# Decoder layer on one core: the second attention's key and value weights split inside the first attention, its first key and value projections at the first attention's end

## The reference, cut to what matters

```python
q = (x @ Wq).reshape(b, t, KV, G, D); k = (x @ Wk).reshape(b, t, KV, D); v = (x @ Wv).reshape(b, t, KV, D)
w = softmax(where(causal_mask, einsum('bqhgd,bkhd->bhgqk', q, k) * scale, -inf))
x2 = norm(x + einsum('bhgqk,bkhd->bqhgd', w, v).reshape(b, t, H * D) @ Wo)
Q = (x2 @ xWq.T + bq).reshape(bs, sl, H, HD)
K = (ctx @ xWk.T + bk).reshape(bs, sl, H, HD); V = (ctx @ xWv.T + bv).reshape(bs, sl, H, HD)
x3 = norm(x2 + einsum('bshg,bsgd->bshd', softmax(einsum('bshd,bsgd->bshg', Q, K)), V) @ xWo.T + bo)
```

## Time and profile before

| | |
|---|---|
| median of 3 runs | 1992.71 us (1992.0 to 1996.39) |
| profiled execution | 1994.85 us |
| its span, first to last instruction | 1992.8 us |
| TensorE busy | 1866.1 us (94%) |
| VectorE, ScalarE, GpSimd busy | 1143.3, 688.5, 262.8 us |
| granted TensorE clock, mean | 0.979 |
| first attention | from 0 to about 343 us |
| second attention | about 343 to 658 us |
| experts | about 658 us to the end |

### The profile page before, as it was taken

How to read it: one execution, slowest core, us unless ns; L and a number is a source line. 1 busy time by engine, 2 the same in 40 slices (tenths; PEclk the granted TensorE clock), 3 DMA queues, 4 the chain that set the end, 5 groups by cost and what they waited for, 6 DMA issues and landing times.

```text
span 1992.8 us, 33389 instructions
## 1 busy us (share of the span) xinstructions
PE 1866.1 (94%) x12784; PEld 1490.7 (75%) x12784; DVE 1143.3 (57%) x1852; ACT 688.5 (35%) x1501; POOL 262.8 (13%) x239
## 2 busy tenths in 40 slices
PE   5999996699996899999999999999999999999997
PEld 4777775578885577777777878777777778787776
DVE  4555554567775445555464565564755655655665
ACT  5556654211211323333332232332422322424321
POOL 2334434233432000000000000000000000000000
PEclk9999998799998899999999999999999999999999
DMA  2011001200000201112020030020120300300011
GB/s 90 22 32 32 21 21 45 89 23 11 21 0 1 90 1 56 45 27 79 11 75 17 13 83 13 6 89 6 39 56 13 83 13 6 88 7 10 9 48 43
DMA packets 38912, 71.51 MB, mean 36 GB/s; under 512 B 7233, under 2 KB 15553, under 8 KB 38081
## 3 DMA queue, kind: packets, MB, share of 16 engines
q1 hardware_dynamic: 38848, 70.63, 11.6%
HBM read 64.85 MB, written 5.77 MB: 35 GB/s over the span
## 4 chain that ended last, share of the span: by engine, by line
PE 57%; DVE 6%; issue 2%; ACT 1%; DVEq 0%; POOLq 0%; POOL 0%
PE pair L1682 10%; PE pair L1684 10%; PE pair L1683 10%; PE y_ps L1682 3%; PE y_ps L1684 3%; PE y_ps L1683 3%; PE pair L1804 2%; PE pair L1805 2%; PE qa_ps L1682 2%; PE qa_ps L1684 2%; PE qa_ps L1683 2%; PE qd_ps L1858 1%; PE qd_ps L1859 1%; PE qa_ps L1696 1%; PE qd_ps L1682 1%
## 5 line engine op out<-in xcount | busy, mean ns | idle before, releaser
L1682 PE MATMUL pair<-XH,GUH 128*128 128x512 f32 (+1 forms) x960 | 376.2, 392 | 0.0
L1684 PE MATMUL pair<-XH,GUL 128*128 128x512 f32 (+1 forms) x960 | 375.4, 391 | 0.0
L1683 PE MATMUL pair<-XL,GUH 128*128 128x512 f32 (+1 forms) x960 | 374.6, 390 | 0.0
L1596 DVE TENSOR_TENSOR h<-pair,sg 128x512 f32<-128x512 f32 (+1 forms) x120 | 82.7, 689 | 382.2 <-ACT sg L1368 382.1
L1368 ACT ACTIVATE sg<-pair 128x512 f32<-128x512 f32 (+1 forms) x120 | 71.6, 596 | 502.5 <-PE pair L1805 406.6
L1684 PEld LDWEIGHTS pair<-XH,GUL 128*128 128x128 f32 (+1 forms) x960 | 171.7, 179 | 47.9
L1683 PEld LDWEIGHTS pair<-XL,GUH 128*128 128x128 f32 (+1 forms) x960 | 171.9, 179 | 47.0
L1682 PEld LDWEIGHTS pair<-XH,GUH 128*128 128x128 f32 (+1 forms) x960 | 171.6, 179 | 47.0
L1270 POOL TENSOR_TENSOR qb_raw<-qb_raw,qb_scale 128x704 f32<-128x704 f32 x8 | 13.9, 1733 | 1039.9 <-DMA qb_scale<-in_gu_scale 1039.9
L1418 DVE TENSOR_TENSOR HL<-h,HH 128x512 fp32r<-128x512 f32 (+1 forms) x120 | 82.9, 691 | 83.7 <-ACT HH L1280 83.7
L264 ACT ACTIVATE p<-s_ps,nm 128x128 f32<-128x128 f32 (+1 forms) x256 | 103.6, 427 | 76.5 <-DVE nm L347 76.5
(11 more groups left out here) (302 smaller groups left out, 4075.6 us busy)
## 6 DMA issues: line engine op xcount, KB each, us to landing
gu_raw<-in_gu SPq DMA_DIRECT2D x20, 512.0 KB, 4.3
wrep<-soft_f SPq DMA_DIRECT2D x64, 128.0 KB
dw_raw<-in_dw SPq DMA_DIRECT2D x10, 512.0 KB, 4.0
xT_raw<-in_xT SPq DMA_DIRECT2D x8, 512.0 KB, 3.8
x_raw<-in_x SPq DMA_DIRECT2D x8, 512.0 KB, 3.6
c_raw<-in_cT SPq DMA_DIRECT2D x8, 512.0 KB, 4.2
out<-xtok SPq DMA_DIRECT2D x4, 1024.0 KB, 4.2
gu_raw<-in_gu SPq DMA_DIRECT2D x10, 384.0 KB, 3.1
```

The costliest lines, as they stand in the source:

```text
L1596: nc.vector.tensor_tensor(h[0:M, b, :], pair[b][1][0:M, :], sg[0:M, b, :], ALU.mult).then_inc(h_rdy, 1)
L1682: mm(out, wh, xh, start=first, stop=False)
L1683: mm(out, wh, xl, start=False, stop=False)
L1684: return mm(out, wl, xh, start=False, stop=last)
```

## The change

Names first. `landing_in` gives a landing buffer and the low half the same memory, so that the subtraction is in place. `Passage` holds what lives through both attentions: the query weights' memory `WQH`, `WQL` (of the first attention, then of the second), the halves `aXH`, `aXL` of x, which become the context's halves `CH`, `CL`, the second attention's key and value weights, its biases, and three PSUM banks, which are `s_ps` in the first and `j_ps` in the second.

- The first attention's main block issues the loads of the second's key and value weights and biases at its start, and in batch 0 rounds and subtracts them. In batch 7 it loads and splits the first context (`split_x(8)`), loads the second attention's query weights and splits them at the block's end.
- TensorE makes the projections n = 0, 1, 2 of batch 0 (`context(n)`) behind the outputs of batch 7, between the two `turn_rows`.
- `cross` has no splitting block any more. Its main block loads and splits the output weights, makes its constants on GpSimd ahead of the biases (`pb` behind the keys' biases), and starts with `project(0, 3)`.

```diff
@@ attention, SyncE, main block
+                if first:
+                    sp.dma_start(way.k_raw[:], A["xwk"]).then_inc(way.l_k, 16)
+                    sp.dma_start(way.v_raw[:], A["xwv"]).then_inc(way.l_v, 16)
+                    for g in range(4):
+                        sp.dma_start(way.qk_bias[32 * g:32 * g + 32, :, :], A["xbqk"]).then_inc(way.l_b, 16)
+                    sp.dma_start(way.v_bias[:], A["xbv"].partition_broadcast(P)).then_inc(way.l_b, 16)
+                sp.wait_ge(proj_done, NPJ * (b + 1))
+                alone(sp, past)
+                if last:
+                    sp.dma_start(xT[:], A["cT"][:, :, 0:S]).then_inc(l_xt, 16)
+                    sp.dma_start(way.q_raw[:], A["xwq"]).then_inc(way.l_q, 16)
+                else:
...
@@ attention, ScalarE
+            def weights_high(landed, high, raw):
+                act.wait_ge(landed, 16)
+                copy(high[:], raw[:]).then_inc(way.high, 1)
...
-                if not last:
-                    split_x(b + 1)
+                split_x(b + 1)
+                if first:
+                    weights_high(way.l_k, way.WKH, way.k_raw)
                 exps(b, 2)
                 o_copy(b, 0)
                 pt_copy(b, 1)
+                if first:
+                    weights_high(way.l_v, way.WVH, way.v_raw)
                 exps(b, 3)
...
                     o_copy(b, 3)
+                    weights_high(way.l_q, WQH, way.q_raw)
                     features_out(b)
@@ attention, VectorE
+            def weights_low(n, high, low, raw):
+                dve.wait_ge(way.high, n + 1)
+                sub(low[:], raw[:], high[:].bitcast(F32)).then_inc(way.low, 1)
...
                 if last:
                     norm_out(b)
                     features_out(b)
+                    weights_low(2, WQH, WQL, way.q_raw)
@@ attention, TensorE
+            def context(n):
+                if n == 0:
+                    pe.wait_ge(way.low, 2)
+                    pe.wait_ge(xl_rdy, B + 1)
+                    pe.wait_ge(exp_done, U * G * B)
+                t = slice(n % 2 * P, n % 2 * P + P)
+                wh, wl = ((way.WKH, way.WKL), (way.WVH, way.WVL))[n // 2]
+                for k in range(KC):
+                    three(s_ps[n][:], XH[:, k, t], XL[:, k, t], wh[:, k, :], wl[:, k, :], k == 0, k == KC - 1)
...
                 outputs(b)
                 if last:
-                    turn_rows(b)
+                    context(0)
+                    turn_rows(b, 0)
+                    context(1)
+                    turn_rows(b, 1)
+                    context(2)
@@ cross
-        splitter.split([(A["xw" + "qkv"[n]], WH[n][:], WL[n][:]) for n in (1, 2, 0)] + [(A["xwo"], WOH[:], WOL[:])],
-                       first_loads, constants)
-        CH, CL = sb("xCH", [P, KC, S], F32R), sb("xCL", [P, KC, S], F32R)
+        CH, CL = way.XH, way.XL
...
             context(1)
+            sp.dma_start(o_raw[:], A["xwo"]).then_inc(way.l_q, 16)
             context(2)
...
-            act.wait_ge(consts, 11)
+            act.sem_inc(ch_rdy, 1)
+            x_high(0)
+            values_out(0, 0)
+            act.wait_ge(consts, 10)
             copy(apart[:], apart_f[:]).then_inc(const_r, 1)
             copy(identR[:], ident[:]).then_inc(const_r, 1)
-            context_high(0)
-            x_high(0)
-            values_out(0, 0)
             values_out(0, 1)
             context_high(1)
+            act.wait_ge(way.l_q, 32)
+            copy(WOH[:], o_raw[:]).then_inc(way.high, 1)
             x_high(1)
...
-            context_low(0)
+            dve.sem_inc(cl_rdy, 1)
+            keys_turned(0, 0)
             x_low(0)
-            keys_turned(0, 0)
             keys_turned(0, 1)
             context_low(1)
             queries_turned(0, 0)
             queries_turned(0, 1)
             values_turned(0)
+            dve.wait_ge(way.high, 4)
+            sub(WOL[:], o_raw[:], WOH[:].bitcast(F32)).then_inc(way.low, 1)
             x_low(1)
...
+            pe.sem_inc(proj_done, 3)
+            for n in range(3, NPJ):
+                project(0, n)
             pe.wait_ge(const_r, 2)
-            for n in range(NPJ):
-                project(0, n)
```

More of the change, by code:

```diff
@@ L80, in __init__ @@
         self.nc = nc
-        self.landed = [ctx.enter_context(nc.semaphore(f"weights_landed{n}")) for n in range(4)]
-        self.loads = [0] * 4
+        self.landed = [ctx.enter_context(nc.semaphore(f"weights_landed{n}")) for n in range(3)]
+        self.loads = [0] * 3
         self.high, self.low = ctx.enter_context(nc.semaphore("split_high")), ctx.enter_context(nc.semaphore("split_low"))
@@ L152, in attention @@
         st, mv, ve, rstd, half = sb("st", [P, 2, 6]), sb("mv", [P, 2, 2]), sb("ve", [P, 2]), sb("rstd", [P, 2]), sb("half", [P, 2])
-        s_ps = [ctx.enter_context(nc.psum_tensor(f"s_ps{i}", [P, 512], F32)) for i in range(3)]
+        s_ps = way.banks
         t_ps = [ctx.enter_context(nc.psum_tensor(f"t_ps{i}", [P, 4, P], F32)) for i in range(3)]
@@ L397, in batch @@
                 maxima(2)
-                if not last:
-                    split_x(b + 1)
+                split_x(b + 1)
+                if first:
+                    weights_low(0, way.WKH, way.WKL, way.k_raw)
                 reciprocals(b, 2)
@@ L402, in batch @@
                 pt_copy(b, 1)
+                if first:
+                    weights_low(1, way.WVH, way.WVL, way.v_raw)
                 maxima(3)
@@ L522, in outputs, with turn_rows @@
                     done.then_inc(wo_done, 1)
[L524 to L532, removed]
+            def turn_rows(b, i):
+                if i == 0:
+                    pe.wait_ge(pt_act, G * (b + 1))
+                    pe.wait_ge(pt_dve, G * (b + 1))
+                pe.wait_ge(xs_rdy, 2 * b + i + 1)
+                for c in range(KC):
+                    done = nc.tensor.transpose(t_ps[i][:, c, :], xs[:, i, c * P:(c + 1) * P], ident[:])
+                done.then_inc(xt_done, 1)
             pe.wait_ge(l_w, 32)
@@ L701, in rows_out @@
                 nc.gpsimd.tensor_copy(xtok[:, bass.ds(2 * b + i, 1), :], xs[:, i:i + 1, :]).then_inc(xtok_rdy, 1)
-            pool.wait_ge(l_b, 80)
+            nc.gpsimd.memset(half[:], -0.5).then_inc(consts, 1)
+            nc.gpsimd.memset(apart_f[:], 0.0).then_inc(consts, 1)
+            pool.wait_ge(consts, 2)
+            for r in range(0, P, 32):
+                for u in range(2):
+                    part = apart_f[r:r + 32, :, u, :]
+                    nc.gpsimd.affine_select(out=part, in_=part, compare_op=ALU.is_ge, fill=NEG, base=(15, -16)[u],
+                                            pattern=[[0, 8], [0, NH]], channel_multiplier=(-1, 1)[u]).then_inc(consts, 1)
+            pool.wait_ge(consts, 10)
+            pool.wait_ge(way.l_b, 80)
             for s in range(2):
                 keys_biased(0, s)
+            nc.gpsimd.memset(PB[:], 0.0).then_inc(consts, 1)
             for s in range(2):
@@ L894, in batch @@
                     keys_turned(b + 1, 0)
+                if first:
+                    dve.wait_ge(consts, 11)
                 probs_turned(b, 0)
@@ L983, in outputs @@
             def outputs(b, i, projected):
+                if isinstance(b, int) and b == 0:
+                    pe.wait_ge(way.low, 4)
                 pe.wait_ge(ol_rdy, 2 * b + i + 1)
```

98 lines of the change are left out of this document (52 added, 46 removed).

## The result

| | before | after |
|---|---|---|
| median (lowest to highest), us | 1992.36 (1989.74 to 1996.39), 4 runs | 1972.19 (1971.09 to 1975.96), 4 runs |
| profiled execution: its time, its span, us | 1994.85, 1992.8 | 1971.45, 1969.7 |

The ratio is 0.990, 95% interval 0.988 to 0.992: about 20 us less, where 17.7 were forecast. Number 1 of the experiments measured the same pair once more and found 16.8 us (1991.22 - 1974.41). The page of after, against the earlier trace rows: TensorE's busy time falls by 5 of the 23 us of span, the others' barely change, so most of the gain is idle time that went.

A forecast was written before the change was run, and what follows sets the result against it. TensorE is busy 94% of the span, with 22.19 us idle at the seam between the attentions. 6.1 + 0.7 - 25.8 + 0.5 + 0.8 = -17.7 us from the median 1992.71 gives 1975.0 us, range 1970.5 to 1980.5.

The forecast's parts named there:

- Batch 0, +6.1: First attention's batch 0: ScalarE's two weight roundings (1.91 us each) and VectorE's value-weight subtraction (2.29) delay it by 6.1 us.
- Batch 7, +0.7: First attention's batch 7: rounding the first context there delays it by 0.7 us.
- The block's end, +2.8: End of first attention's block: 2.8 us later, VectorE making the query weights' low half (2.29 us) after the last copies.
- Scores by GpSimd's queue: Second attention's start: first scores wait for GpSimd's constants and biases, 13.4 us, and start at 359.4 before batch delays.
- term (a): Seam: GpSimd slowed beside VectorE's subtractions of two SBUF operands; bounds 0 and 1.0 us, 0.5 taken.
- VectorE's cover of 1.5 us: Behind the first scores: VectorE finishes transpose, output weights' low half and subtraction 1.5 us before it needs the scores' result.
- Term (b), the clock, 0.8 us: TensorE's clock may fall at new pauses in batch 0 and before the first scores; bounds 0 and 2.65 us, 0.8 taken.
- From there on nothing of the change is met again: After the second attention's first scores: no further effect, so the sum is made for their start.
- the splits were not hidden: Rival for batch 0: the splits are hidden, the 6.1 us fall away, 1969 us; chance 0.06.
- clock falls in both new gaps: Rival: pauses in batch 0 and at the seam each cost a 2.65 us restart, (a) whole, 1980 us; chance 0.11.
- the seam did not stay: Rival: first scores still wait for something at the old instant, time stays near 1993 us; chance 0.03.
- the middle batches, from the third on, kept full clock: Against the slower rival: second attention's steady batches lose the clock, 14 restarts cost 37 us, 2012 us; chance 0.03.

The follow-up runs named there:

- Number 1: The changed kernel measured again with no edit: 1974.41 us, ratio 0.991 to the kernel before.
- Number 3: Changed kernel with the value weights' low half on VectorE moved behind group 3's maxima in batch 0: 1971.06 us, ratio 0.991 to before.
- number 5: Changed kernel with GpSimd's memset of pb moved behind the query biases of batch 0: 1969.62 us, ratio 0.989 to before.
- number 4: Changed kernel with only addresses changed, the context's halves 672 bytes off the key and value weights' alignment: 1976.00 us, ratio 0.993 to before.
- number 7: Changed kernel with only addresses changed, second attention's x and output halves at the weights' offset within 4 KB: 1971.49 us, ratio 0.991 to before.
- number 6: Changed kernel with key and value weights rounded at batch 0's end and subtracted in batch 7, in idle time: 1967.56 us, ratio 0.989 to before.
- number 2: Changed kernel with the three projections put back at the second attention's start: 1979.69 us, ratio 0.994 to before.
- 8: Changed kernel with the edits of numbers 5, 6 and 7 together: 1961.65 us, ratio 0.986 to before.

## Why the prediction was right

The sign, the size and the cause hold: 1972.19 us against 1975.0, inside the range. Step by step, each at its place in the profile:

- **Batch 0, +6.1.** Right: group 3's exponentials start 6.06 us later (53.11 against 47.05) in the second execution of the changed kernel, 5.71 in the first; counted from group 1's exponentials, 5.8 in both. Number 3 confirms the part of VectorE's subtraction (2.29), and shows that the 0.71 us of waiting that I had left out of the sum were to be had there.
- **Batch 7, +0.7.** Right in kind, smaller in size: 0.46 us in number 3, where the clock did not fall (from batch 6's first output matmul to batch 7's last, 298.50 to 339.09 against 295.41 to 335.54).
- **The block's end, +2.8** (2.7 by its own terms, 345.6 - 342.88). Right: from the start of the last output matmul to GpSimd's next block 356.81 - 346.45 = 10.4 us, forecast 345.9 - 335.54 = 10.4.
- **Scores by GpSimd's queue.** Right in kind: they start 0.1 us behind its second query bias, and number 5, which takes the memset out of the queue ahead of them, moves them. In size: 371.27 - 356.81 = 14.5 us, forecast 13.5 and 0.5 for term (a). The selects took 3.78 instead of 2.69, so (a) was its upper bound of 1.0 and not the middle. The prediction had that case too, by the rule of the Trainium skill (GPSIMD Engine Reference, section 1, Specifications) that GpSimd's SBUF interfaces are shared with VectorE and contended by its instructions with two SBUF inputs; the trace agrees with it.
- **VectorE's cover of 1.5 us** held: its next maxima wait for the scores, and not behind the output weights:

```profile
371.14 2.26 DVE L870 TENSOR_TENSOR xWoL<-xWoL_raw,xWoH 128x2048 fp32r<-128x2048 f32 x1
...
376.70 0.69 DVE L900 TENSOR_REDUCE xtop<-so_ps 128x16 f32<-128x512 f32 x1 [2.17 <-PE so_ps L1036]
```

- **Term (b), the clock, 0.8 us: the step that failed ahead of the scores.** In after 7.74 us (68.38 against 60.64) had been lost by the first output matmul of batch 0, where the splits explain 5.71: 2.0 from the clock. Of the 3.2 us lost from there to the last output matmul of batch 7, number 3, whose clock did not fall, lost 0.77: 2.4 from the clock. Together 4.4 us. I looked for a fall at the seam, and the seam kept full clock over 1.76 us; I did not think of batch 7 at all. In the pause before the first scores the clock did fall (0.53 of full from 369 to 380 us), but before has a fall at its scores too (0.57 from 386 to 394 us), and from the first scores to the second batch the two take nearly the same time, 34.6 and 34.8 us. The loss isn't fixed: 1.5 us in number 1 (8.35 - 6.06 - 0.77), none in number 3. That the change causes the falls in batch 7 is not shown (last section). The rival "clock falls in both new gaps" had the price nearly right and one of its two places wrong.
- **"From there on nothing of the change is met again": the other step that failed.** The change moved the context's halves to other addresses, and each middle batch became 0.31 us shorter: an estimate of 2.2 us in seven batches. That addresses do this is shown by numbers 4 and 7. The rest of the 9.1 us behind the scores is mostly the clock, which changes from one execution to the next of one program.

With the clock's 4.4 for 0.8, 1.0 for 0.5, and 5.71 for 6.1, the sum for the first scores is 385.23 - 17.7 + 3.6 + 0.5 - 0.4 = 371.2, measured 371.27. In the median the losses ahead and the gains behind nearly cancel: that the forecast came out nearer than its terms is luck.

The rivals: the splits were not hidden (number 6 shows what that would have brought), the seam did not stay, and the middle batches, from the third on, kept full clock in every profiled execution; number 1 shows one fall between the second and third.

## What to carry to other kernels

Where one stage waits for loads and conversions that depend on nothing, do them in the stage before; but ask of every engine's queue which instruction there is waited for, since the first place that is free in the program may be in a batch whose engines have no slack there. Once the seam closes, read the queue of the engine that used to be idle under it, here GpSimd's constants. And when tensors move, compare the dense stretches that "nothing touches": a new address changed each matmul by 2 to 3% here.

## What was not expected of the hardware

- **Addresses and matmul spacing.** At full clock the dense 512-column matmuls of the second attention start 0.2335 us apart or 0.2265 to 0.2276 (the first step of a group left out), with the same program of TensorE. Which of them depended on where the two operands lay: fast when the tensors of both had the same offset modulo 4096 bytes per partition (context in after and number 7, x and outputs in number 7 alone), slow at an offset of 672 bytes (context in before and number 4) and of 2592 (outputs in after). Equal offsets are not needed: by the same reckoning the first attention's output operands lie 1536 bytes apart in before, and 22 steps up to the row at 335.54 take 5.01 us, 0.2277 each.

```profile
330.53 0.39 PE L442 MATMUL j_ps<-WOL,OH 128*128 128x512 f32 x1
```

  Which modulus or distance decides was not tried, nor whether the values' step (4.25, 4.20, 4.08 us) goes by the same cause.
- **GpSimd beside VectorE.** The eight selects took 2.69 us before and in number 2, and 3.78 or 3.77 beside a subtraction of two SBUF tensors; two value biases 2.51 and 3.53. VectorE pays too: in number 5 the context's subtraction took 2.35 us instead of 1.23.

```profile
360.71 2.35 DVE L870 TENSOR_TENSOR aXL<-c_raw,aXH 128x1024 fp32r<-128x1024 f32 x1 [3.35 <-ACT aXH L803]
```

- **The clock after the same wait.** TensorE waited 2.87 us in batch 0 of after and 2.86 in number 1; the clock fell in the first and not in the second. Of the six profiled executions with this wait it fell there in five, and in none of the four without it (before, 3, 6 and 8). The Trainium skill (TensorE: Matmul & The Clock Gate, part 1) says that the instants of change shift from run to run, and these two executions agree. In the first attention's batch 7 it fell in six of the nine kernels that round the context there, partly others than those of batch 0; what decides there stays open. The waits there are no longer than before's: TensorE waited 1.52, 0.97 and 1.17 us in after, where the clock fell, and 1.75, 0.97 and 1.18 us in before, where it did not. So that the change causes the falls in batch 7 is not shown.
